# Two heads in the two halves of the partitions: float32r query and key parts for the shared-key and layer 2 attention

## The chip, the cores and the metric

The kernel runs on one core of one Trainium2 chip. The metric is the device time of one execution in microseconds (us); the median of some runs is compared.

## The reference, cut to what matters

A network of four layers works on x of 1024 tokens by 256 features, in float32. Three of its attentions are causal softmax attentions with 16 heads of 16 features: the latent attention of layer 0 (with rotated parts, 80 features per head), the shared-key attention beside it, and the attention of layer 2. The change touches the last two:

```python
# layer 0, feed-forward place: one key head for all query heads
att = einsum('bhqd,bkd->bhqk', q, k_shared) * (1.0 / sqrt(hd))
att = softmax(where(causal, att, -inf)); y = einsum('bhqk,bkd->bhqd', att, v_shared)
# layer 2
scores = einsum('bhqd,bhkd->bhqk', q, k) * scale
attn = softmax(where(causal, scores, finfo.min)); out = einsum('bhqk,bhkd->bhqd', attn, v)
```

## The kernel before, in words

Tokens are 8 tiles of 128 (T = 1024, P = 128, NT = 8, HALF = 512); a group is 4 heads (GH = 4, HD = 16). Groups 0 to 3 are the latent attention, 4 to 7 the shared-key one, 8 to 11 layer 2's. Each group goes through these steps.

- Row maxima. For each tile of queries TensorE makes approximate scores, queries on the PSUM partitions, keys along the bank (`maxima_unit`, L1553), adds a causal mask of bf16 with an identity (L1555), and VectorE reduces the bank (`row_maxima`, L1109). `MAX_UNITS` lists these units of at most 512 columns: 38 per group, with 4 heads of 128, 2 heads of 256 or 1 head of more columns. During attention they take turns in the 2 banks of psD; outside it (WIDE) in 4 banks. The negated maxima are transposed (L1561), copied (`mrow`, `mrowb`) and loaded by a DMA as one more row of the queries, against a row of ones in the keys.
- Scores. For each tile kt of keys, `score_units` makes the transposed scores of the 4 heads into psA (2 units of 2 banks, `scores_T`, L1571; the latent attention has a second product, L1570). For kt below 4 a unit is one head with both halves of the queries; from 4 on it is two heads with one half. ScalarE takes the exponential of each unit into Pr (L855, L860), GpSimd clears the triangle on the diagonal for the whole kt (`mask_exponentials`, L730).
- Values product. Four heads stand in four column groups of the array (`values_product`, L1608), one kt behind the scores. ScalarE copies psO to OT (L875) at the end of a group, TensorE transposes it (L1619), and VectorE divides and stores (`outputs`).

The maxima of group g are made beside the scores of groups g-1 and g-2, some units after each score unit or values product (`beside`, `some_maxima`), all of group 4's beside group 3. For groups 0 and 8 they are made ahead. TensorE works its list in order, so it waits where a bank isn't drained.

For groups 4 to 11 each query or key value is cut in three bf16 thirds (`split` on VectorE, `split_step` on GpSimd: copy, subtract, copy, subtract; L1101 to L1104), stored to DRAM (`d_gq`, `d_gk`, `d_q2`, `d_k2`), and loaded as 6 stacked products of parts, 96 rows, by `load_group`. The sixth-part order is

```python
Q_PARTS = (0, 0, 0, 1, 1, 2)
K_PARTS = (0, 1, 2, 0, 1, 0)
STACK = len(Q_PARTS) * HD
```

The latent attention keeps float32r parts (Qr, Kr), and its maxima read only the high bf16 halves of them (`high`). SyncE issues all DMAs in one order: group loads wait for the last scores of the group whose place they take.

## Time and profile before

| | |
|---|---|
| runs (3), us | 1019.24, 1023.3, 1026.06; median 1023.3 |
| profiled execution: span from first to last instruction | 1016.6 us (its own time isn't given beside the span) |
| TensorE busy | 868.2 us (85%) |
| VectorE, ScalarE, GpSimd busy | 572.4, 381.3, 225.2 us |
| mean granted TensorE clock | 0.910 of full |
| groups end (copy of psO begins), us | 199.74, 250.56, 302.16, 347.51, 381.48, 420.18, 454.16, 481.36; layer 2: 736.90, 770.75, 801.86, 823.16 |

### The profile page before, as it was taken

The page shows a single profiled execution, that of the slowest core. Times are in us where ns is not written, and L with a number is a line of the kernel's source. Part 1 is how long each engine was busy: PE and PEld are TensorE (multiplying, and loading weights), DVE is VectorE, ACT ScalarE, POOL GpSimd, SP SyncE. Part 2 cuts the span into 40 slices and gives each one's busy share as a digit, 9 for nine tenths or more (in the row PEclk, how much of TensorE's full clock was granted, in tenths as well). Part 3 has the DMA queues.
Part 4 walks back from the last instruction along what each step waited for, and adds up shares of the span by engine and source line. Part 5 has one row for each costly group of instructions (what it writes and reads, how often), then busy time and mean ns, then how long its engine had stood idle before and what let it go on. Part 6 is the DMA issues. An engine that isn't in the chain of part 4 may idle for free.

```text
span 1016.6 us, 11900 instructions
## 1 busy us (share of the span) xinstructions
PE 868.2 (85%) x4799; PEld 506.2 (50%) x4799; DVE 572.4 (56%) x986; ACT 381.3 (38%) x470; POOL 225.2 (22%) x207
## 2 busy tenths in 40 slices
PE   4991979788899999988589998978999889969897
PEld 2451335444455433334237877623333257868776
DVE  4871656363647777832543345396777427954452
ACT  2410014424243555465242331214555763410331
POOL 2541422401010234111210100400111227810010
PEclk9975679989899999999687998966999989989799
DMA  5599446374833400001500002477100051000001
GB/s 170 194 200 195 198 83 116 66 123 122 128 53 100 64 1 1 2 1 33 183 0 1 1 1 86 103 146 106 23 2 1 1 196 63 1 1 1 1 1 42
DMA packets 33313, 71.32 MB, mean 70 GB/s; under 512 B 5637, under 2 KB 14413, under 8 KB 33254
## 3 DMA queue, kind: packets, MB, share of 16 engines
q1 hardware_dynamic: 33258, 70.56, 30.1%
q8 instruction: 38, 0.62, 0.3%
q14 instruction: 17, 0.14, 0.0%
HBM read 49.27 MB, written 18.48 MB: 67 GB/s over the span
## 4 chain that ended last, share of the span: by engine, by line
PE 63%; DVE 19%; DMA 6%; ACT 5%; issue 4%; SPq 2%; POOL 1%; ACTq 0%; DVEq 0%; POOLq 0%
PE psD L1489 10%; PE psO L1608 10%; PE psO L1489 10%; PE psA L1489 9%; PE psD L1553 9%; DVE mx L1109 8%; PE psA L1571 7%; PE psA L1570 3%; DMA Kr<-d_kn 2%; DVE hid_low L1403 2%; SPq L460 2%; PE psD L1555 2%; ACT Pr L855 2%; PE psA L1521 1%; DVE Kg L1391 1%
## 5 line engine op out<-in xcount | busy, mean ns | idle before, releaser
L1109 DVE TENSOR_REDUCE mx<-psD 128x1 f32<-128x512 f32 (+3 forms) x416 | 258.0, 658 | 157.5 <-PE psD L1555 133.1
L855 ACT ACTIVATE Pr<-psA 128x1024 f32<-128x1024 f32 (+3 forms) x192 | 161.5, 865 | 167.5 <-PE psA L1571 167.0
L730 POOL TENSOR_SCALAR_AFFINE_SELECT Pr<-Pr 128x512 f32<-128x512 f32 x96 | 61.1, 636 | 402.8 <-ACT Pr L855 323.7
L860 ACT ACTIVATE Pr<-psA 128x1024 f32<-128x1024 f32 (+3 forms) x96 | 63.3, 702 | 60.3 <-PE psA L1571 59.9
L1608 PE MATMUL psO<-Pr,Vh 128*32 128x512 f32 (+3 forms) x768 | 80.3, 498 | 3.6 <-POOL Pr L730 3.0
L1553 PE MATMUL psD<-Kr,Qr 80*128 80x512 bf16 (+3 forms) x167 | 51.3, 360 | 35.7 <-issue 20.5
L1555 PE MATMUL psD<-maskq,identb 128*128 128x128 bf16 x349 | 72.5, 232 | 0.0
L1571 PE MATMUL psA<-Qr,Kr 113*128 113x512 f32 (+3 forms) x192 | 67.8, 359 | 0.0
L1553 PE MATMUL psD<-Kg,Qs 96*128 96x512 bf16 (+3 forms) x192 | 57.2, 331 | 5.3 <-DVE mx L1109 2.0
L1553 PE MATMUL psD<-Ks,Qs 96*128 96x512 bf16 (+3 forms) x166 | 54.5, 358 | 4.6 <-DVE mx L1109 3.7
L1553 PEld LDWEIGHTS psD<-Kr,Qr 80*128 80x128 bf16 x167 | 17.1, 105 | 75.6 <-issue 29.5
L1571 PE MATMUL psA<-Qs,Ks 97*128 97x512 bf16 (+3 forms) x192 | 46.7, 337 | 3.9 <-ACT Pr L855 3.3
L1521 PE MATMUL psA<-identf,xn 128*128 128x128 f32 x96 | 21.7, 389 | 31.5 <-DVE xn L1077 31.1
L1571 PE MATMUL psA<-Qs,Kg 97*128 97x512 bf16 (+3 forms) x192 | 44.9, 326 | 3.8 <-ACT Pr L855 3.3
L1553 PEld LDWEIGHTS psD<-Kg,Qs 96*128 96x128 bf16 x192 | 18.1, 96 | 54.9 <-DVE mx L1109 43.5
L1608 PE MATMUL psO<-Pr,Vg 128*32 128x512 f32 (+3 forms) x384 | 40.1, 497 | 2.0 <-POOL Pr L730 1.3
L1570 PE MATMUL psA<-Qr2a,Kr 128*128 128x512 f32 (+3 forms) x96 | 38.8, 418 | 3.2 <-issue 2.7
L1553 PEld LDWEIGHTS psD<-Ks,Qs 96*128 96x128 bf16 x166 | 16.7, 102 | 47.4 <-DVE mx L1109 41.5
L1571 PEld LDWEIGHTS psA<-Qr,Kr 113*128 113x128 f32 x192 | 38.0, 198 | 2.7
L1555 PEld LDWEIGHTS psD<-maskq,identb 128*128 128x128 bf16 x349 | 36.7, 105 | 4.9 <-issue 1.4
L1570 PE MATMUL psA<-Qr2b,Kr 128*128 128x512 f32 (+3 forms) x96 | 37.3, 402 | 0.6 <-ACT Pr L855 0.6
L1521 PEld LDWEIGHTS psA<-identf,xn 128*128 128x128 f32 x96 | 16.6, 195 | 35.5 <-issue 23.5
(392 smaller groups left out, 1730.0 us busy)
## 6 DMA issues: line engine op xcount, KB each, us to landing
d_qr<-Pr SPq DMA_DIRECT2D x16, 512.0 KB, 3.6
Qr<-d_qr SPq DMA_DIRECT2D x4, 1024.0 KB
Qr2a<-d_qr SPq DMA_DIRECT2D x4, 1024.0 KB, 24.9
Qr2b<-d_qr SPq DMA_DIRECT2D x4, 1024.0 KB, 19.9
Pr<-d_cb SPq DMA_DIRECT2D x8, 512.0 KB, 9.0
Qr<-d_qn SPq DMA_DIRECT2D x12, 256.0 KB, 13.6
Kr<-d_kn SPq DMA_DIRECT2D x12, 256.0 KB, 16.9
Qs<-d_gq SPq DMA_DIRECT2D x24, 128.0 KB
```

What stands on the lines that cost most here:

```text
L460: sp.dma_start(dst, src).then_inc(s, 16)
L730: pool.affine_select(out=block_, in_=block_, pattern=[[0, GH], [1, P]], compare_op=ALU.is_ge, fill=0.0, base=0, channel_multiplier=-1).the ...
L855: act.activation(place[:, h, q0:T], src[:, q0:T], ACT.Exp, scale=score_scale(i)).then_inc(a_drained, 1)
L860: act.activation(place[:, h:h + 2, q0:T], src[:, :, q0 - HALF:HALF], ACT.Exp, scale=score_scale(i)).then_inc(a_drained, 1)
L1109: dve.tensor_reduce(mx[:, j, part, h0:h0 + nh], src, AX, ALU.max).then_inc(d_drained, 1)
L1489: op = pe.matmul(dst, lhsT, rhs, start=start and k == 0, stop=stop and k == len(terms) - 1)
L1521: op = pe.transpose(dst[:, tile_cols(j)], src[:, j, c * P:(c + 1) * P], identf[:])
L1553: op = pe.matmul(dst[:, k * w:(k + 1) * w], q, kk, start=True, stop=not diagonal)
L1555: op = pe.matmul(dst[:, (k + 1) * w - P:(k + 1) * w], identb[:], maskq[:], start=False, stop=True)
L1570: pe.matmul(out_, second[0], second[1](lo, (half + 1) * HALF), start=True, stop=False)
L1571: op = pe.matmul(out_, k, q(lo, (half + 1) * HALF), start=second is None, stop=not (diagonal and mask))
L1608: op = pe.matmul(psO[h * VW:(h + 1) * VW, lo:hi], values(i, kt, h), e, start=kt == 0, stop=kt == last_kt, tile_position=(0, h * VW), skip_ ...
```

## The change

Queries and keys of groups 4 to 11 are kept as two float32r parts (ScalarE copies the value twice out of PSUM, once rounded to float32r; one subtraction gives the low part), and stacked three times (high by high, high by low, low by high): 48 rows, 49 with the row of maxima. Even heads stand in partitions 0 to 48, odd heads in 64 to 112. The shared key is held twice, once in each half. A score unit is now two heads (one of each half) and one half of the queries, each head in its own bank, for every kt. A maxima unit holds heads of one partition half only: the list for these groups is `PAIR_UNITS`, 40 units, heads alternating between halves. Maxima read the high bf16 halves of the float32r parts. The mask is added by two matmuls with 64 rows and 64 columns each from `mask64`, in the head's partition half. Stores to DRAM are two of 512 KB per tile in place of one of 768 KB; group loads have as many bytes, in rows of 4 KB in place of 2 KB; ones and maxima rows are loaded once for each half. The maxima row is float32r.

```diff
-Q_PARTS = (0, 0, 0, 1, 1, 2)
-K_PARTS = (0, 1, 2, 0, 1, 0)
+Q_PARTS = (0, 0, 1)
+K_PARTS = (0, 1, 0)
+ROWS = P // 2
+def pair_units():
+    for j in range(NT):
+        for part in range(1 + (j >= NT // 2)):
+            w = min(HALF, (j + 1) * P) if part == 0 else (j + 1) * P - HALF
+            for heads in ((0, 2), (1, 3)) if w <= 2 * P else ((0,), (1,), (2,), (3,)):
+                yield j, part, heads, w
...
-            o = ((i % 4) * GH + h) * T
-            return t[:].bitcast(BF16)[0:rows, o + a:o + b]
+            r, o = ROWS * (h % 2), ((i % 4) * GH // 2 + h // 2) * T
+            return (Qr if t is Qs else Kr)[r:r + rows, o + a:o + b]
...
+            for a in range(2):
+                load(mask64[a * ROWS:(a + 1) * ROWS, :, :],
+                     ins["c_maskk"].bitcast(BF16).rearrange("(c r) q -> r c q", c=2), consts_in)
...
                 def parts(t, d, order):
-                    for r, part in enumerate(order):
-                        load(t[:].bitcast(BF16)[r * HD:(r + 1) * HD, o:o + GH * T].rearrange("p (h t) -> p h t", h=GH),
-                             d[part, rows, :].rearrange("(h d) t -> d h t", d=HD), s)
+                    for a in range(2):
+                        for r, part in enumerate(order):
+                            at = a * ROWS + r * HD
+                            load(t[at:at + HD, o:o + n].bitcast(F32).rearrange("p (k t) -> p k t", k=GH // 2),
+                                 d[part, rows, :].rearrange("(k a d) t -> a d k t", a=2, d=HD)[a], s)
...
+            def store_parts(d, rows, u, n):
+                low, high_part = split_place(u)
+                for part, place in enumerate((high_part, low)):
+                    load(d[part, rows, :], place[0:rows.stop - rows.start], split_stored[n])
...
             def split(u, filled, rows=P, done=split_done):
                 pool.wait_ge(a_drained, filled)
-                for k in range(4):
-                    split_step(u, k, rows, done)
+                v, high_part = split_place(u)
+                pool.tensor_tensor(v[0:rows].bitcast(F32R), v[0:rows], high_part[0:rows], ALU.subtract).then_inc(done, 1)
...
-                        if kt < NT // 2:
+                        if kt < NT // 2 and not is_mla(i):
+                            for half in range(2):
+                                lo = max(q0, half * HALF)
+                                for h in range(0, GH, 2):
+                                    src = take().rearrange("p (h t) -> p h t", h=2)
+                                    act.activation(place[:, h:h + 2, lo:(half + 1) * HALF],
+                                                   src[:, :, lo - half * HALF:HALF], ACT.Exp,
+                                                   scale=score_scale(i)).then_inc(a_drained, 1)
...
+            def split_unit(u, rows=P):
+                src = take()[0:rows, :]
+                low, high_part = split_place(u)
+                act.activation(low[0:rows], src, ACT.Copy)
+                act.activation(high_part[0:rows].bitcast(F32R), src, ACT.Copy).then_inc(a_drained, 1)
...
-                link(dve.tensor_copy(b[:, 0], v))
-                link(dve.tensor_tensor(v, v, b[:, 0], ALU.subtract))
-                link(dve.tensor_copy(b[:, 1], v))
-                dve.tensor_tensor(b[:, 2], v, b[:, 1], ALU.subtract).then_inc(split_done, 1)
+                v, high_part = split_place(u)
+                dve.tensor_tensor(v.bitcast(F32R), v, high_part, ALU.subtract).then_inc(split_done, 1)
...
+            def maxima_unit(i, j, part, heads, w):
+                dst = d_unit()
+                rows = MLA if is_mla(i) else STACK
+                diagonal = part == (j >= NT // 2)
+                for k, h in enumerate(heads):
+                    q = high(head_rows(Qs, i, h, rows, j * P, (j + 1) * P))
+                    kk = high(key_rows(i, h, rows, part * HALF, part * HALF + w))
+                    end = (k + 1) * w
+                    op = pe.matmul(dst[:, k * w:end], q, kk, start=True, stop=not diagonal)
+                    if diagonal and is_mla(i):
+                        op = pe.matmul(dst[:, end - P:end], identb[:], maskq[:], start=False, stop=True)
+                    elif diagonal:
+                        half = slice(ROWS * (h % 2), ROWS * (h % 2 + 1))
+                        for c in range(2):
+                            at = end - P + c * ROWS
+                            op = pe.matmul(dst[:, at:at + ROWS], mask64[half, c, :], identb[half, half],
+                                           start=False, stop=c == 1)
...
+                def pair(unit):
+                    half, first = unit
+                    dst = a_unit()
+                    for b, h in enumerate((first, first + 1)):
+                        op = scores_T(dst, b * HALF, key_rows(i, h, rows, kt * P, (kt + 1) * P),
+                                      lambda lo, hi: head_rows(Qs, i, h, rows, lo, hi), kt, half)
+                    op.then_inc(a_filled, 1)
+
+                if not is_mla(i):
+                    return [(half, h) for half in range(kt * P // HALF, 2) for h in range(0, GH, 2)], pair
```

## Rows read from the trace of the kernel before

**Rows 1.** The page, the chain that ended last: shares of the span by engine.
```profile
PE 63%; DVE 19%; DMA 6%; ACT 5%; issue 4%; SPq 2%; POOL 1%; ACTq 0%; DVEq 0%; POOLq 0%
```

**Rows 2.** Windows: from:to, length, busy us of each engine (x instructions), granted clock, DMA share, GB/s.
```profile
347.50:381.50 34.00, 31.41 (x234) 12.35 (x233) 25.68 (x45) 19.41 (x27) 10.75 (x16) 1.00 0.17 22
692.50:736.90 44.40, 40.43 (x270) 16.40 (x270) 31.99 (x54) 24.93 (x30) 5.09 (x8) 0.90 0.50 73
801.90:823.20 21.30, 17.96 (x142) 5.35 (x142) 6.57 (x9) 15.38 (x23) 5.09 (x8) 1.00 0.00 1
677.60:692.00 14.40, 12.30 (x41) 3.78 (x41) 12.93 (x24) 0.00 (x0) 0.00 (x0) 0.50 0.15 58
765.90:771.66 5.76, 5.27 (x37) 2.09 (x36) 5.49 (x10) 4.79 (x6) 0.64 (x1) 1.00 0.00 0
```

**Rows 3.** The chain by line, first in group 4 (347.5:381.5), then in group 3 (302.2:347.5).
```profile
by line: PE psO L1608 24.3%; PE psD L1553 22.1%; DVE mx L1109 17.7%; PE psA L1571 15.5%; PE psD L1555 3.9%; POOL Pr L730 3.8%; PE psD L1619 3.4%; ACT Pr L860 3.2%; issue 2.5%; ACT Pr L855 2.4%; PE psD L1561 0.8%; DVE mneg L1114 0.8%; POOLq 
...
by line: PE psD L1553 24.9%; PE psO L1608 19.6%; PE psA L1571 16.6%; PE psA L1570 14.6%; DVE mx L1109 13.3%; DMA Qs<-d_gq 11.7%; PE psD L1555 5.5%; PE psD L1619 2.6%; issue 1.0%; PE psD L1561 0.2%
```

**Rows 4.** Timeline of VectorE in group 10: start, us, line [idle before, releaser].
```profile
773.39 1.89 DVE L1109 TENSOR_REDUCE mx<-psD 128x1 f32<-128x512 f32 x3 [0.63 <-PE psD L1553]
```

**Rows 5.** Timeline of TensorE in group 5: maxima, mask, then one values product.
```profile
382.49 0.22 PE L1553 MATMUL psD<-Kg,Qs 96*128 96x128 bf16 x1
382.55 0.22 PE L1555 MATMUL psD<-maskq,identb 128*128 128x128 bf16 x1
382.69 1.06 PE L1608 MATMUL psO<-Pr,Vg 128*32 128x512 f32 x8
```

**Rows 6.** Instructions by line and form: busy us, mean ns of one, idle before.
```profile
L1571 PEld LDWEIGHTS psA<-Qr,Kr 113*128 113x128 f32 x192 | 38.0, 198 | 2.7
...
L1571 PEld LDWEIGHTS psA<-Qs,Kg 97*128 97x128 bf16 x192 | 15.6, 98 | 22.2 <-ACT Pr L855 10.1 <-issue 2.8 <-ACT Pr L860 1.7
...
L1571 PE MATMUL psA<-Qr,Kr 113*128 113x128 f32 x32 | 8.2, 275 | 0.0
...
L1571 PE MATMUL psA<-Qs,Kg 97*128 97x128 bf16 x32 | 5.3, 221 | 1.9 <-ACT Pr L855 1.8
```

**Rows 7.** Timeline of TensorE at 38.9, at 514.4 and at 266.3 us.
```profile
38.90 0.50 PE L1489 MATMUL psO<-lat_parts,wq_low 64*128 64x512 f32 x1
39.33 0.50 PE L1489 MATMUL psO<-lat_parts,wq_high 128*128 128x512 f32 x1
...
514.42 0.23 PE L1774 MATMUL psD<-K,Q 32*128 32x128 bf16 x1
514.58 0.23 PE L1777 MATMUL psD<-maskq,identb 128*128 128x128 bf16 x1
...
266.33 0.39 PE L1570 MATMUL psA<-Qr2a,Kr 128*128 128x512 f32 x1
266.56 0.39 PE L1571 MATMUL psA<-Qr,Kr 113*128 113x512 f32 x1
```

**Rows 8.** The chain before group 8, and ScalarE's timeline there (the last row).
```profile
642.62 1.24 DVE Pr L1102
...
649.72 3.44 DMA d_k<-Pr
...
653.59 0.43 SPq L460
...
659.72 7.32 DMA Ks<-in_c_ones4b
...
644.27 1.02 ACT L822 ACTIVATE Pr<-psA 128x1024 f32<-128x1024 f32 x1 [2.41 <-PE psA L1489]
```

**Rows 9.** Windows in which the DMAs are full: 2 KB rows, then 4 KB rows.
```profile
654.00:666.00 12.00, 7.58 (x45) 6.61 (x44) 7.07 (x19) 3.93 (x10) 8.38 (x5) 0.91 1.06 149
194.00:205.00 11.00, 5.30 (x28) 3.37 (x26) 0.00 (x0) 5.71 (x6) 3.39 (x4) 0.92 1.01 165
```

More of the change, by code:

```diff
@@ L74, in max_units, with units_of @@
                 yield j, part, h0, nh, w
-MAX_UNITS = list(max_units())
+MAX_UNITS = [(j, part, tuple(range(h0, h0 + nh)), w) for j, part, h0, nh, w in max_units()]
+def pair_units():
[4 more added lines that the diff above has]
+                yield j, part, heads, w
+PAIR_UNITS = list(pair_units())
+def units_of(g):
+    return MAX_UNITS if g < NG else PAIR_UNITS
 MAX_END = 5
@@ L159, in build @@
         mrow = sb("mrow", [GH * NT, P])
-        mrowb = sb("mrowb", [GH * NT, P], BF16)
+        mask64 = sb("mask64", [P, 2, P], BF16)
         rec = sb("rec", [P, 4, GH])
@@ L337, in maxima_of, with rows_in @@
             return 2 * NG + 1 if i == "L1" else maxima(i)
+        ROW_DMAS = [1] * NG + [2] * NG + [1] + [2] * NG
+        def rows_in(count):
+            return 16 * sum(ROW_DMAS[:count])
         A_GROUP = 4 * GH + 4 * GH // 2
@@ L535, in maxima_row @@
                 else:
-                    o = (i % 4) * GH * T
-                    load(Qs[:].bitcast(BF16)[STACK:STACK + 1, o:o + GH * T], mrowb[:], mrow_in)
+                    o, n = (i % 4) * GH // 2 * T, GH // 2 * T
+                    for a in range(2):
+                        at = a * ROWS + STACK
+                        load(Qr[at:at + 1, o:o + n].bitcast(F32), mrow[a * n // P:(a + 1) * n // P, :], mrow_in)
             for p in range(H // 2):
@@ L749, in _ @@
                     mask_exponentials(i, kt)
-                    if i == 0:
-                        split_step(kt // 4, kt % 4)
+                    if i == 0 and kt % 4 == 0:
+                        split(kt // 4, A["gq"])
                     n = NT * (i - NG) + kt
@@ L953, in _ @@
                 if u == 3:
[L954 to L955 removed]
+                    act.wait_ge(split_stored[0], 32 * 2)
+                split_unit(3 + u)
             act.wait_ge(v_cleared, 4)
@@ L1183, in attention @@
                             maxima_row(nxt)
-                        row_maxima(beside(groups, i, kt)[1])
+                        row_maxima(*beside(groups, i, kt))
                         if kt == 1 and i - 1 in groups:
@@ L1540, in value_units @@
                         last.then_inc(d_filled, 1)
-            def maxima_unit(i, j, h0, nh, w, part):
+            def maxima_unit(i, j, part, heads, w):
                 dst = d_unit()
                 rows = MLA if is_mla(i) else STACK
-                for k in range(nh):
-                    h = h0 + k
-                    q = head_rows(Qs, i, h, rows, j * P, (j + 1) * P)
-                    kk = key_rows(i, h, rows, part * HALF, part * HALF + w)
-                    if is_mla(i):
-                        q, kk = high(q), high(kk)
-                    diagonal = part == (j >= NT // 2)
-                    op = pe.matmul(dst[:, k * w:(k + 1) * w], q, kk, start=True, stop=not diagonal)
-                    if diagonal:
-                        op = pe.matmul(dst[:, (k + 1) * w - P:(k + 1) * w], identb[:], maskq[:], start=False, stop=True)
+                diagonal = part == (j >= NT // 2)
[12 more added lines that the diff above has]
+                                           start=False, stop=c == 1)
                 op.then_inc(d_filled, 1)
@@ L1632, in attention @@
                     arrived(groups[0])
-                    for j, part, h0, nh, w in MAX_UNITS:
-                        maxima_unit(groups[0], j, h0, nh, w, part)
+                    for unit in units_of(groups[0]):
+                        maxima_unit(groups[0], *unit)
                     maxima_transpose(groups[0], GH)
```

138 lines of the change are left out of this document (64 added, 74 removed).

## The prediction

> **What bounds the kernel now.** I read the page's chain that ended last first: TensorE holds 63% of it and VectorE 19% [rows 1]. Then I cut the attention into its groups of four heads, each ending with the copy of psO by ScalarE. Groups 0 to 3 are the first attention, 4 to 7 the shared-key one, 8 to 11 layer 2. In [rows 2] the reader is to see that no engine fills a group: group 4 takes 34.0 us with VectorE busy 25.7 and ScalarE 19.4, and group 9 repeats it (33.8 us); groups 5, 6, 7 and 10 (38.7, 34.0, 27.2 and 31.2 us by the table of their ends) are of the same make with other work beside.
>
> The chain inside group 4 says who is late: values products (L1608) 24.3%, maxima matmuls (L1553) 22.1%, VectorE's maxima 17.7%, scores (L1571) 15.5%, masks (L1555) 3.9% [rows 3]. So scores are 5.3 us of a group's 34.0, maxima matmuls 7.5, masks 1.3. Nor is the time one kind of time. The first eighth of a group (kt 0) lasts 5.76 us with VectorE busy 5.49: there nothing but VectorE counts. After it VectorE waits 0.6 us at a time for TensorE to come back from a values product [rows 4]. That is the time a faster TensorE can take.
>
> **Overlap of the halves.** Now a score matmul uses 97 rows, one head at a time; after, 49 rows of one half, the next head in the other half, into another PSUM bank. No row of before shows two matmuls on different rows of the array. The nearest show them on different columns: eight values products of 512 columns, four heads at a time, end within 1.06 us, and 128 columns alone keep a matmul 0.22 us [rows 5]; so tiles do run together. The bounds: a pair costs as much as one (5.3 us become about 2.7 per group), or as much as two (no gain). I take the first, by that row, with 0.2 us lost because a float32r score is up to 54 ns longer than a bf16 one (275 against 221 ns at 128 columns [rows 6], less where more columns hide the weight load): -2.5 us. Maxima matmuls alternate halves too, but only 2 psD banks take turns and VectorE empties them, so two of them seldom meet; one can run beside half of a score pair. Between 0 and -2.5 us (a third of 7.5); I take -0.8, since VectorE takes most of that back.
>
> **What the same groups lose.** (a) 32 diagonal heads per group get two mask matmuls of 64 columns for one of 128. Mask and maxima matmuls of 128 columns start 0.06 us apart [rows 5]; two halves cost between nothing more and 0.06 each, so 0 to 1.9 us per group; I take 0.2, as columns rule in all the rows. (b) Maxima read high halves in steps of four bytes; no row parts that from the rest, so I bound it at 0 and 5% of their 7.5 us, and take 0.2. (c) Tile mode. A switch is seen at both ends of a values product: its first matmul starts 0.14 us after a mask matmul, where 0.06 is usual [rows 5]. These switches stay. Where 128-row and 64-row float32r matmuls alternate, starts are 0.43 us apart at 512 columns [rows 7], against 0.23 between two float32r matmuls of 128 and 113 rows; where bf16 matmuls of 32 and 128 rows alternate, 0.16 us against 0.06 [rows 7]. So a switch costs 0.1 us, 0.2 when a float32r weight load follows. The output transposes (128 rows) now stand between 64-row work: two switches, +0.3. (d) Float32r weight loads last 198 ns, bf16 ones 98 [rows 6]; behind a short mask matmul they show, +0.3. (e) Two more maxima units, 40 for 38: +0.2. Sum of losses 1.2 us, so group 4, 5 and 9 gain 2.1 each: -6.3. After it VectorE's 25.7 us plus its waits are next late; at 31.9 us there is room. Group 8 has the same scores, but more of it is VectorE's (32.0 of 44.4 us [rows 2]): -2.0. Groups 6 and 10 have fewer maxima to fill: -1.2 each. Groups 7 and 11 have none; there a score follows each values product directly and pays the float32r switch (about 0.1 us, 6 to 9 times), and the chain runs through ScalarE and GpSimd: -0.3 each.
>
> On that weight load the Trainium skill (TensorE: Matmul & The Clock Gate, Weight-path perf modes) speaks against the change: fast weight load is on for 128 weights of a type other than FP32. The trace agrees in direction, by the 198 against 98 ns. And (TensorEngine Tiling (Array Packing), Key Properties) it says that a change of tiling mode drains TensorE; the trace agrees, with the 0.43 us starts. Neither page prices the two; by the rows they are the 0.3 and 0.3 us of (c) and (d), and without them the sum would be some 4 us lower.
>
> **Group 3.** It scores the first attention (113 and 128 rows) while it makes the maxima of group 4. These maxima now have 48 rows, so each of some 15 changes from maxima to scores costs 0.15 more (a float32r load after a switch, less the 0.05 paid already) and some 14 back 0.1: 3.6 us. Part of it falls where TensorE waits for a bank anyway. +2.5; the bounds are 0 and 3.6, and it is TensorE that leads this chain (L1553, L1608, L1571 and L1570 hold 76% [rows 3]).
>
> **Around the groups.** Before group 8 the chain runs through four VectorE steps for each of two tiles, which end at 649.7 us, the store of d_k2 (3.44), 12 loads issued at some 0.45 us each, and the landing at 667.0 [rows 8]. After: ScalarE copies twice (1.02 us more), VectorE subtracts once. ScalarE takes the second tile from 644.3 on, and two copies and one step of 1.24 us end near 644.3 + 2.1 + 1.2 = 647.6: -2.1. The stores grow from 0.75 to 1.0 MB: +0.7. One more load of ones and a second DMA for the maxima row, each 0.4 of issue: +0.8. The loads carry the same bytes but 4 KB rows for 2 KB; in stretches where the DMAs are full, 4 KB rows moved 165 GB/s and 2 KB rows 149 [rows 9], so the 13.4 us of loading shrink by 1.3 (between 0 and 3). Together -1.9. VectorE's run of 38 maxima after it is as long as before, within 0.2. The load of group 4, waited for in group 3 (11.7% of its chain [rows 3]), gains by the same rate, -0.5. GpSimd's splits of four steps become one subtraction; in group 0, where they stand between the selects, I count nothing, since selects hold under 4% of a chain [rows 3]. The two loads of mask64 are issued ahead of the first projections and hidden by x and the norm. The longer ScalarE drains (two copies) sit under TensorE's 3.4 us per unit.
>
> **Sum.** -6.3 - 2.0 - 2.4 - 0.6 + 2.5 - 1.9 - 0.5 = -11.2 us. The span of 1016.6 becomes 1005.4. The profiled execution's own time isn't shown beside the span; the median of the runs is 1023.3, 6.7 us more, so I add 6.7: 1012.1 us.
>
> **Rivals.**
> A, turns: the two halves do not run together. For it: no row shows row tiles together. Against it: the column tiles [rows 5]. Place: every score pair. Then a strong group pays the 1.2 us of losses and 0.6 for longer float32r scores instead of gaining: +1.8 in 4, 5, 8 and 9, +1.3 in 6 and 10, +1.0 in 7 and 11, +2.5 in group 3, -2.4 around: +11.9, 1035 us, slower. It decides from the point where a pair of 512 columns costs more than one and a half matmuls.
> B, weight loads in turn: the halves stream together but float32r loads do not. At 128 columns the float32r score lasts 275 ns against 221 [rows 6], which is the load showing. Eight of a group's 24 pairs have 256 columns or fewer and four have 384; they would cost some 0.1 and 0.05 more, 1.0 per group in six groups: 1018 us.
> C, the clock: where TensorE is fed at VectorE's pace, the granted clock is 0.50, the 1.2 GHz level (677.6 to 692.0 us [rows 2]), and it stays so into group 8. If less TensorE work lets it fall in the VectorE-bound start of groups too, each fall costs about 3 us (half of TensorE's share of some 6 us), six times: 1030 us. Against it: group 11, with TensorE least busy, keeps 1.00, the 2.4 GHz level [rows 2].
> D, more overlap: maxima matmuls hide as well, and groups fall to VectorE's time plus 4.5 us of waits, 30 us; -3.8 in three groups, as much in proportion elsewhere, and 4 KB rows pay fully: 1001 us.
> That the change does nothing of what it says is A.
>
> **Chances.** The sum 0.47 (1006 to 1018), A 0.12, B 0.14, C 0.12, D 0.15. The range of 999 to 1031 leaves out most of A and the tail of D. A measurement here can tell about 1%, from 1013.1 to 1033.5. Faster by more: D, two thirds of the sum's case and little of B, 0.49. Slower: A and a tail of C, 0.13. Within: 0.38.
>
> **What would show it.** Right: two L1571-like matmuls starting within 0.02 us in different halves; scores under 9% of a strong group's chain; groups 4 and 9 near 32 us; group 3 near 48 us without its DMA wait shrinking much; group 8's first maxima near 665 us; a few tenths of a microsecond between 64-row and 128-row matmuls in group 3. Wrong: pairs starting 0.2 us apart (A), pairs of 128 columns 0.2 us apart (B), clock under 1.00 in groups 4 to 7 (C). The forecast is most open in how much of the overlap VectorE gives back, and in group 3.

## The result and the profile after

The changed kernel takes 1082.1 us, median of 4 executions (1076.9 to 1089.3), beside 1023.8 for the kernel before: ratio 1.059, 95% interval 1.055 to 1.062. The profiled span is 1087.5 us against 1016.6, 70.9 more; it is that of the longest of the four executions, so it lies further from before than the medians do, which are 58 apart. The prediction of 1012 has the wrong sign, and 1082 is outside its range of 999 to 1031. In this document medians are over all executions of a kernel, and ratios over those that lie near its fastest, because a kernel whose clock dips scatters by several per cent.

The page of the changed kernel: TensorE's row of busy time, then the clock in 40 slices, then the chain by engine, which answers to [rows 1].

```profile
PE 929.4 (85%) x5055; PEld 543.8 (50%) x5055; DVE 567.6 (52%) x996; ACT 388.1 (36%) x477; POOL 205.1 (19%) x192
...
PEclk9985789898999566789688998855656888989898
...
PE 66%; DVE 16%; DMA 6%; ACT 5%; issue 4%; SPq 2%; POOL 1%; DVEq 0%; ACTq 0%
```

The row to read is PEclk: from slice 14 on, in the shared-key groups, it shows 5 to 8 for the most part where the groups of before had 1.00 throughout, and again in layer 2. Windows of the changed kernel, columns as in [rows 2]: group 4, group 8 from 1.8 us behind its first score (the window of before in [rows 2] begins 0.6 us ahead of that score, so the two lengths don't compare), group 9, group 11, then key tile 1 and key tile 4 of group 4.

```profile
356.43:402.35 45.92, 43.43 (x267) 19.15 (x265) 26.55 (x46) 19.42 (x27) 10.72 (x16) 0.57 0.12 16
733.00:785.58 52.58, 49.13 (x304) 21.67 (x302) 32.73 (x55) 23.04 (x29) 5.09 (x8) 0.56 0.45 57
785.58:831.15 45.57, 43.23 (x267) 19.56 (x265) 26.55 (x46) 19.39 (x27) 5.08 (x8) 0.57 0.01 1
865.20:890.77 25.57, 21.18 (x142) 6.87 (x142) 6.57 (x9) 15.44 (x22) 5.09 (x8) 0.80 0.00 1
357.33:367.87 10.54, 10.40 (x55) 4.45 (x54) 5.80 (x12) 3.57 (x6) 1.94 (x3) 0.50 0.42 53
381.98:385.19 3.21, 3.06 (x34) 1.38 (x34) 2.34 (x5) 1.93 (x4) 2.50 (x4) 1.00 0.00 0
```

Group 4 takes 45.9 us instead of 34.0 while VectorE (26.6 us busy for 25.7) and ScalarE have almost the same work as before. TensorE is busy 43.4 of it, and its granted clock is 0.57, the mean of stretches at 0.50 (1.2 GHz) and at 1.00 (2.4 GHz). Key tile 1 runs wholly at 0.50 with TensorE busy 10.40 of 10.54 us; key tile 4, at 1.00, takes 3.2 us. Group 11, at 1.00 before, has 0.80.

The same by line, group 4 first, then group 3, beside [rows 3].

```profile
by line: PE psO L1644 34.8%; PE psD L1571 26.0%; PE psA L1595 15.5%; DVE mx L1131 10.2%; PE psD L1578 4.9%; PE psD L1655 4.1%; ACT Pr L867 2.2%; issue 1.6%; PE psD L1585 0.6%; DVE mrow L1148 0.6%; DVE mneg L1136 0.6%; DVEq L1065 0.1%
...
by line: PE psD L1571 22.9%; PE psA L1594 18.1%; PE psO L1644 17.8%; DVE mx L1131 15.7%; PE psA L1595 13.6%; DMA Qr<-d_gq 10.8%; PE psD L1578 4.6%; PE psD L1655 2.3%; issue 1.6%; DVE mrow L1148 0.6%; PE psD L1585 0.2%; DVEq L1065 0.1%
```

The values products (L1644), which the change does not touch, go from 24.3% of 34.0 us to 34.8% of 45.9, from 8.3 us to 16.0: the mark of a slower clock, not of more work. VectorE's share falls from 17.7% to 10.2%. TensorE bounds the group.

The overlap itself is there. TensorE's timeline in key tile 4 of group 4, at the full clock: four score products of 384 columns, in two pairs, are over in 0.60 us; in the kernel before, four in turn took 0.81 (fourth row). But it does not reach short products: four of 128 columns in two pairs take 0.44 us (fifth row, group 7 of the changed kernel), four in turn took 0.39 (last row, group 4 of before).

```profile
384.37 0.41 PE L1571 MATMUL psD<-Kgr,Qr 48*128 48x512 bf16 x2
384.61 0.23 PE L1578 MATMUL psD<-identb,mask 64*128 64x64 bf16 x4
384.67 0.60 PE L1595 MATMUL psA<-Qr,Kgr 49*128 49x384 f32 x4
...
368.65 0.81 PE L1571 MATMUL psA<-Qs,Kg 97*128 97x384 bf16 x4
...
514.43 0.44 PE L1595 MATMUL psA<-Qr,Kgr 49*128 49x128 f32 x4
...
374.52 0.39 PE L1571 MATMUL psA<-Qs,Kg 97*128 97x128 bf16 x4
```

By the copies of psO, the 70.9 us of span lie so: groups 4, 5 and 9 +12.0, +11.3 and +11.7; group 8 from its first score to its end +10.5; group 3 +5.4; groups 6, 7, 10 and 11 +2.0, +2.3, +2.9 and +4.3; the way from group 7 to group 8's first score +1.7; groups 0 to 2 +3.5 and all behind group 11 +3.3. The 3.5 us come and go from kernel to kernel: that of experiment 5, which leaves these groups as they were, has 3.7 of them.

The way into group 8 in the chain, beside [rows 8], and the window in which its loads fill the DMAs, beside the first of [rows 9].

```profile
685.12 3.55 DMA d_k<-Pr
...
694.80 9.86 DMA Kr<-onesf
...
705.35 21.88 DVE mx L1131 x40
...
729.05 2.15 DMA Qr<-mrow
```

```profile
690.00:704.00 14.00, 8.84 (x53) 7.77 (x52) 4.49 (x21) 4.33 (x11) 2.35 (x1) 0.90 1.06 143
```

From the end of the last split (684.7 us; 649.7 before), when the first of the two stores is issued, to the landing of the loads (704.7; 667.0) it is 19.9 us, 17.3 before. With 4 KB rows the loads moved 143 GB/s, with 2 KB rows 149.

### The profile page after: what moved, and what is told of

Its sections match the earlier page's. It is cut to its first block, busy times and chain, and to the rows that moved or that the text cites. A ratio compares the mean times of both kernels' runs of the same rounds, so it can differ in the third digit from the quotient of the medians.

```text
span 1087.5 us, 12430 instructions
## 1 busy us (share of the span) xinstructions
PE 929.4 (85%) x5055; PEld 543.8 (50%) x5055; DVE 567.6 (52%) x996; ACT 388.1 (36%) x477; POOL 205.1 (19%) x192
## 4 chain that ended last, share of the span: by engine, by line
PE 66%; DVE 16%; DMA 6%; ACT 5%; issue 4%; SPq 2%; POOL 1%; DVEq 0%; ACTq 0%
PE psO L1644 13%; PE psD L1509 10%; PE psD L1571 9%; PE psA L1509 9%; PE psO L1509 9%; DVE mx L1131 7%; PE psA L1595 7%; PE psA L1594 3%; DMA Kr<-d_kn 2%; SPq L465 2%; DVE hid_low L1423 2%; ACT Pr L867 2%; PE psA L1541 1%; PE psD L1578 1%; DMA Pr<-d_cb 1%
## 5 line engine op out<-in xcount | busy, mean ns | idle before, releaser
L1131 DVE TENSOR_REDUCE mx<-psD 128x1 f32<-128x512 f32 (+4 forms) x432 | 264.2, 643 | 210.9 <-PE psD L1573 88.2
L1571 PE MATMUL psD<-Kr,Qr 80*128 80x512 bf16 (+7 forms) x335 | 121.5, 414 | 45.9 <-issue 21.9
L1595 PE MATMUL psA<-Qr,Kr 49*128 49x512 f32 (+7 forms) x384 | 130.6, 470 | 6.2 <-ACT Pr L867 4.4
L1571 PEld LDWEIGHTS psD<-Kr,Qr 80*128 80x128 bf16 (+1 forms) x335 | 34.4, 106 | 140.1 <-DVE mx L1131 60.1
L1644 PE MATMUL psO<-Pr,Vh 128*32 128x512 f32 (+3 forms) x768 | 99.9, 606 | 2.8 <-POOL Pr L740 2.3
L1595 PEld LDWEIGHTS psA<-Qr,Kr 113*128 113x128 f32 (+1 forms) x384 | 69.3, 225 | 24.4 <-ACT Pr L867 11.6
L1571 PE MATMUL psD<-Kgr,Qr 48*128 48x512 bf16 (+3 forms) x192 | 68.8, 411 | 7.8 <-DVE mx L1131 4.3
L1595 PE MATMUL psA<-Qr,Kgr 49*128 49x512 f32 (+3 forms) x192 | 58.4, 553 | 4.3 <-ACT Pr L867 3.5
L1644 PE MATMUL psO<-Pr,Vg 128*32 128x512 f32 (+3 forms) x384 | 55.7, 670 | 1.7 <-POOL Pr L740 1.3
L1578 PE MATMUL psD<-identb,mask 64*128 64x64 bf16 x480 | 56.8, 220 | 0.0
L1578 PEld LDWEIGHTS psD<-identb,mask 64*128 64x128 bf16 x480 | 48.9, 116 | 14.9 <-issue 8.2
L1509 PE MATMUL psA<-xnT,WA 128*128 128x512 f32 x56 | 30.9, 712 | 2.2 <-ACT xnT L832 2.2
```

Source lines behind the costliest of these rows:

```text
L1131: dve.tensor_reduce(mx[:, j, part, max_slots(i, heads)], src, AX, ALU.max).then_inc(d_drained, 1)
L1509: op = pe.matmul(dst, lhsT, rhs, start=start and k == 0, stop=stop and k == len(terms) - 1)
L1571: op = pe.matmul(dst[:, k * w:end], q, kk, start=True, stop=not diagonal)
L1578: op = pe.matmul(dst[:, at:at + ROWS], mask64[half, c, :], identb[half, half], start=False, stop=c == 1)
L1595: op = pe.matmul(out_, k, q(lo, (half + 1) * HALF), start=second is None, stop=not (diagonal and mask))
L1644: op = pe.matmul(psO[h * VW:(h + 1) * VW, lo:hi], values(i, kt, h), e, start=kt == 0, stop=kt == last_kt, tile_position=(0, h * VW), skip_ ...
```

## The experiments

Fifteen kernels ran, one of them twice. Each is a small edit of one of the two kernels; "clock" is the granted clock of whole groups in the windows of its trace.

**1. Score pairs in turn.** The pair takes two heads of one half.

```diff
-                    for b, h in enumerate((first, first + 1)):
+                    for b, h in enumerate((first // 2, first // 2 + 2)):
```

> The changed kernel, but the two score products of a pair take heads (0,2) or (1,3), which lie in the same half of the partitions, so that they run one behind the other; products, columns, maxima and masks are the same, and ScalarE writes the same numbers. Theory A (the clock falls because the pairs run at once and leave TensorE too lightly loaded): the granted clock of groups 4, 5, 8 and 9 returns from 0.56 to 0.64 towards 1.0, and the time falls from 1082 to 1025 to 1050 us although the overlap is lost. Theory B (the clock falls because the maxima use half of the rows, whatever the scores do): the clock stays at 0.55 to 0.65 and the time rises by the lost overlap, 5 us a group at the lower level, to 1095 to 1120. Theory C (the time is in mode switches and weight loads, the clock is a symptom): time up by 2.5 us a group, about 1100.

1132.5 us, ratio 1.107 (1.099 to 1.114). The clock in groups 4, 5 and 6 was 0.57, 0.67 and 0.69, group 4 took 48.3 us. So the overlap is not what lowers the clock (theory A falls), and the kernel is 50 us slower without it. That is not the overlap alone: group 4, at 0.57 with and without it, loses 2.4 us, while groups 6, 10 and 11 also have a lower clock than in the changed kernel (0.69, 0.67 and 0.56 against 0.88, 0.85 and 0.80).

**2. Full-array work ahead of each pair.**

```diff
                     dst = a_unit()
+                    for c in range(4):
+                        pe.matmul(dst[:, c * P:(c + 1) * P], identb[:], maskq[:], start=True, stop=True)
```

> The changed kernel with idle work added: ahead of each score pair TensorE multiplies four full 128 x 128 tiles by 128 columns into the bank that the pair then overwrites, 192 times 0.23 us = 44 us of TensorE at the full clock, 89 us at the lower one. Nothing is left out. The clock theories (A or B): the full-array work lifts the granted clock of groups 4, 5, 8 and 9 above 0.85, so their 45 to 50 us go to 36 to 42 and the whole kernel does not get slower, 1050 to 1085 us, with 44 us of TensorE work more. Rival C (mode switches and TensorE work bound it): the clock stays near 0.6 or does not matter, and the time goes up by 45 to 90 us, 1125 to 1170.

1153.9 us (1126.5 to 1166.9). Groups 4 and 5 in the windows of an execution of 1162.7 us:

```profile
358.85:412.63 53.78, 51.87 (x364) 24.40 (x363) 26.76 (x48) 19.98 (x27) 10.68 (x16) 0.70 0.08 11
412.63:458.30 45.67, 43.23 (x371) 21.35 (x369) 30.71 (x57) 19.87 (x26) 14.78 (x14) 0.97 0.01 2
```

Neither reading was wholly right. The time is where rival C put it; the clock did not stay near 0.6 everywhere: one group holds 0.97, the next falls to 0.62, and TensorE's added work costs more than the clock gives back. In this trace group 5, at 1.00 in its first key tile, keeps it, while groups 4 and 6 are down to 0.50 by key tile 1 and stay there for two key tiles or more.

**3. Maxima over 112 rows.** The masks are whole again too; the score pairs still run at once.

```diff
-                rows = MLA if is_mla(i) else STACK
+                rows = MLA if is_mla(i) else ROWS + STACK
...
+                    hh = h if is_mla(i) else h - h % 2
```

> The changed kernel, but the maxima products contract 112 rows instead of 48: rows 48 to 63, filled with the second parts by one DMA more for each of the tiles, and the other half are taken in, so each product is of two heads together and the maxima are not the reference's; the masks are 128 x 128 again. The score pairs still run at once. Theory A (the overlap of the scores pulls the clock down): the clock stays at 0.6 to 0.75, time 1055 to 1085 us. Theory B (the half-array maxima do): the clock of groups 4, 5, 8 and 9 is above 0.9 and the time near 1020 to 1035. Theory C (switches): four switches a key tile fewer, 1060 to 1075 with the clock as low as before.

> The changed kernel with maxima products of 112 rows, once more, for its trace: 1051 us again. Theory B (the half-array maxima hold the clock down): groups 4, 5 and 9 at a granted clock of 0.9 or more, so that what is left of the loss, 29 us, is float32r weight loads, turns between tiles at the scores, and the lead-in to group 8. Theory A (the score pairs hold it down as well): still 0.6 to 0.8 in some of these groups.

1051.4 us, ratio 1.027 (1.024 to 1.031); one of its four executions took 3713.7 us, of which more at the end. The kernel was run once more and took 1047.7, and the windows are of that execution. Groups 4 and 9:

```profile
356.70:392.53 35.83, 33.68 (x235) 12.58 (x233) 26.27 (x47) 19.47 (x26) 10.74 (x16) 1.00 0.13 21
762.40:798.15 35.75, 33.70 (x235) 12.55 (x233) 26.27 (x47) 19.39 (x26) 5.07 (x8) 1.00 0.01 2
```

With full-array maxima and masks the clock is back at 1.00, although the pairs still run in half tiles (groups 7 and 11, without maxima, have 0.86 and 0.89). Theory B holds for the larger part of the loss. And a second finding: at the full clock group 4 still takes 35.8 us, 1.9 more than before.

**4. Half-array maxima in the kernel before.**

```diff
-                rows = MLA if is_mla(i) else STACK
+                rows = MLA if is_mla(i) else 48
...
+                            op = pe.matmul(dst[:, at:at + 64], mask64[0:64, c, :], identb[0:64, 0:64],
```

> The kernel before, but its maxima products contract the first 48 of the 96 rows, and the mask products are in two parts of 64 rows as in the changed kernel; the scores are the old ones of 97 rows, one head at a time. Maxima leave out the second and third parts of the query. Theory A (only overlapped scores pull the clock down): clock 0.95 to 1.0 in groups 4, 5 and 9, time 1025 to 1040 us. Theory B (half-array maxima do): clock 0.55 to 0.7 in groups 4, 5, 8 and 9, time 1070 to 1090. Theory C (switches between row tiles of 64 and 128 cost the time): 1045 to 1060 with the clock near 1.0.

1128.3 us (1102.9 to 1138.6), though the scores are the old ones. Groups 4 and 10 of the execution of 1102.9 us:

```profile
357.69:409.81 52.12, 50.70 (x268) 15.91 (x267) 26.65 (x45) 19.77 (x27) 10.66 (x16) 0.63 0.09 12
833.49:883.23 49.74, 48.03 (x217) 13.31 (x216) 18.55 (x32) 19.52 (x26) 5.10 (x8) 0.56 0.00 1
```

Cause and effect from the other side: half-array maxima with their cut masks, put into the old kernel, cost 81 us at its fastest and 106 at the median. They do not lower the clock everywhere: groups 5 and 6 of this trace have 1.00.

**5. Few rows, or the half tile?** Maxima of 65 rows in the kernel before.

```diff
-                rows = MLA if is_mla(i) else STACK
+                rows = MLA if is_mla(i) else 65
```

> The kernel before, but its maxima products contract the first 65 of the 96 rows: one row more than half of the array, so that they remain products of a 128-row tile beside the scores of 97 rows, and no mask is cut in two. Left out of the maxima: the second and third parts of the query. Theory B1 (few active rows in the maxima keep the clock low; 48 rows did): 65 rows do some of it, granted clock below 0.9 in at least two of the groups 4, 5, 8, 9, 10 and 1040 to 1090 us. Theory B2 (what keeps the clock low is the half-array row tile and what comes with it, the turns between 64-row and 128-row tiles): clock 1.0 in groups 4, 5, 9 and 10 and 1020 to 1026 us, as before.

1024.7 us, ratio 1.004 (1.001 to 1.007), group 4 in 33.99 us at 1.00. Leaving out a third of the rows does no harm as long as the products are no half tiles. A bound between 48 and 65 active rows that had nothing to do with tiles would look the same; no run parts these two.

**6. No half tiles at all.** Maxima and scores over 112 rows.

```diff
+                        hh = h - h % 2
+                        op = scores_T(dst, b * HALF, key_rows(i, hh, ROWS + STACK, kt * P, (kt + 1) * P),
```

> The changed kernel with no 64-row tile in the shared-key and layer 2 attention: maxima and scores contract 112 rows, of two heads together, one product behind the other, so the output is not the reference's; columns, exps, transfers and the float32r operands of the scores are those of the changed kernel. Theory B (64-row tiles hold the clock down): groups 4, 5, 8, 9 and 10 at 1.0 as before, 1018 to 1035 us, the rest over 1022 being float32r weight loads and the lead-in to group 8. Rival (float32r score products, with their 4-byte operands, hold it down): clock 0.6 to 0.8 and 1055 to 1090 us.

1044.0 us, ratio 1.023 (1.018 to 1.027), clock 1.00 in groups 4, 5, 6 and 9; group 4 takes 35.84 us. The first theory is right on the clock, but the time is above the 1035 that it allowed. In group 4 it ties with the 112-row kernel of experiment 3, in which the pairs run at once (35.83 us). So there the overlap gains nothing over full tiles in turn. TensorE's timelines show why. First the kernel of experiment 5, whose scores are those of before, then this one, that of experiment 3 and that of experiment 7 below, each with a maxima product, the pair, and the next maxima product:

```profile
349.31 0.39 PE L1553 MATMUL psD<-Kg,Qs 65*128 65x512 bf16 x1
349.54 0.60 PE L1571 MATMUL psA<-Qs,Kg 97*128 97x512 bf16 x2
349.97 0.90 PE L1553 MATMUL psD<-Kg,Qs 65*128 65x512 bf16 x2
...
436.88 0.39 PE L1578 MATMUL psD<-Kgr,Qr 112*128 112x512 bf16 x1
436.91 0.82 PE L1596 MATMUL psA<-Qr,Kgr 112*128 112x512 f32 x2
437.57 0.40 PE L1578 MATMUL psD<-Kgr,Qr 112*128 112x512 bf16 x1
...
435.55 0.39 PE L1578 MATMUL psD<-Kgr,Qr 112*128 112x512 bf16 x1
435.87 0.49 PE L1596 MATMUL psA<-Qr,Kgr 49*128 49x512 f32 x2
436.30 0.40 PE L1578 MATMUL psD<-Kgr,Qr 112*128 112x512 bf16 x1
...
439.48 0.39 PE L1578 MATMUL psD<-Kgr,Qr 112*128 112x512 bf16 x1
439.80 0.73 PE L1596 MATMUL psA<-Qr,Kgr 49*128 49x512 f32 x2
440.46 0.40 PE L1578 MATMUL psD<-Kgr,Qr 112*128 112x512 bf16 x1
```

From one maxima product to the next it is 0.66 us with bf16 scores in turn, 0.69 with float32r scores of 112 rows in turn, 0.75 with half tiles at once, and 0.98 with half tiles in turn. So among half tiles the overlap does gain: the next product starts 0.43 us after a pair at once and 0.66 after a pair in turn. But half tiles in turn between full-tile products cost 0.29 more than full tiles in turn (0.98 - 0.69), and the overlap gives 0.23 of that back.

**7. Only the scores in half tiles, in turn** (experiments 1 and 3 together).

> The changed kernel with maxima products of 112 rows (two heads together) and the score pairs taken from one half, so that half-array products still run, but only the scores, and in turn. Theory B (what holds the clock down is any stretch in which one half-array product runs at a time): the granted clock of groups 4, 5, 8, 9 falls to 0.55 to 0.8 and the time is 1070 to 1110 us. Rival (the scores alone are too small a share of TensorE's time, or the turns between full and half tiles let it recover): clock 0.95 to 1.0, and the time is 1048 us plus the lost overlap, 3 us in each of eight groups: 1062 to 1075 us.

1089.9 us, ratio 1.063 (1.056 to 1.070). Clock 1.00 in groups 4 and 5 but 0.63 in group 7, which has scores and values products only:

```profile
354.49:393.42 38.93, 36.46 (x234) 14.72 (x233) 26.35 (x47) 19.60 (x26) 10.73 (x16) 1.00 0.12 18
474.13:514.55 40.42, 38.00 (x175) 16.73 (x174) 4.65 (x10) 15.50 (x22) 5.07 (x8) 0.63 0.03 10
```

Against experiment 3, running at once is worth 3.1 us in group 4 (38.93 against 35.83). Theory B expected a lower clock in groups 4, 5, 8 and 9, and they have 0.83 to 1.00; the rival's time, up to 1075, is passed, in part because groups 7 and 11 fall (0.63 and 0.81). Half-array scores, too, lower the clock where no full-array maxima stand between them.

**8. A burst of full-array work at key tile 1.**

```diff
+                    for _ in range(64 * (kt == 1 and unit == (0, 0))):
+                        pe.matmul(dst[:, 0:P], identb[:], maskq[:], start=True, stop=True)
```

> The changed kernel with 64 full-array products of 128 x 128 x 128 ahead of the first score pair of key tile 1 in each of the groups 4 to 11, 3.7 us at the full clock and 6.8 us at the lower one; their results are overwritten. Theory B (nothing but a stretch of full-array work lifts the clock, and the half-array maxima only fail to lift it): the clock returns during the burst and stays for the rest of the maxima, key tiles 1 to 3 of group 4 take 17 us in place of 24.7, groups 4, 5 and 9 take 40 to 43 us in place of 46 to 50, and the whole 1055 to 1080 us. Rival (half-array maxima pull a full clock down again within a key tile): clock back at 0.50 in key tile 2, groups 50 us or more, whole 1110 to 1140 us.

1085.5 us, ratio 1.060 (1.053 to 1.067): as the changed kernel, and between the two forecasts. Four windows of group 4, of about a key tile each, cut at the first exp of each; the burst is in the first:

```profile
350.04:360.57 10.53, 9.75 (x103) 7.16 (x102) 5.75 (x10) 4.90 (x6) 1.34 (x2) 0.84 0.94 144
360.57:367.63 7.06, 6.28 (x60) 2.94 (x57) 5.56 (x11) 3.56 (x5) 1.34 (x2) 1.00 0.01 3
367.63:372.73 5.10, 4.62 (x42) 1.86 (x38) 4.35 (x8) 3.15 (x4) 0.00 (x0) 1.00 0.01 2
372.73:378.48 5.75, 5.48 (x34) 2.01 (x34) 3.42 (x7) 2.62 (x4) 1.34 (x2) 0.70 0.00 0
```

Full-array work does lift the clock, and half-array maxima pull it down again: 0.70 in key tile 3 here, 0.57 in key tile 2 of the next group. The second and third rows are the changed kernel at the full clock: 7.06 and 5.10 us, where the kernel before, cut in the same way, has 7.37 and 5.16. Key tile 4 follows at 1.00 as well, with 3.15 us against 3.70. That is what the change gains there when the clock holds: 0.9 us in three of the eight key tiles.

**9. One maximum for two heads.** Half of the maxima units, over 112 rows and with whole masks as in experiment 3.

```diff
-            for heads in ((0, 2), (1, 3)) if w <= 2 * P else ((0,), (1,), (2,), (3,)):
+            for heads in ((0, 2),) if w <= 2 * P else ((0,), (2,)):
```

> The changed kernel, but what the softmax subtracts is, for the two heads of a pair, the maximum of the sum of their scores: one maxima product of 112 rows for two heads, half as many products, masks and row maxima, and the negated maxima written twice. The row maxima of each head by itself are left out; the softmax divides the same factor out again, so the output stays near the reference's while that sum does not lie far below a head's own scores. Expected by the full-clock reading of the 112-row kernel (1048 us): TensorE loses 8 us of maxima products and 3 us of masks in each of eight groups, and VectorE 10 us; ScalarE's 19 to 20 us a group and the values products are left. Groups of 36 us become 27 to 30 us, the lead-in to group 8 loses 10 us: 975 to 1000 us, under both kernels. Theory A (half-tile scores alone hold the clock down once the full-array maxima get fewer): clock 0.6 to 0.8 and 1020 to 1050 us.

1010.4 us, ratio 0.986 (0.978 to 0.994), one or two per cent under before but above the forecast. Two executions took 1004 us and one 1017; the fourth took 1309.5, with a mean granted clock of 0.548, so this kernel isn't safe from a long fall of the clock either. Group 4 takes 32.1 us at 0.89 and group 6 34.8 at 0.84: the clock still dips in an ordinary execution. It is no drop-in: what it subtracts is the maximum of a sum of two heads' scores, which bounds neither head, and the exp can overflow on other data.

**10 and 11. Which part of the half-array maxima?** Maxima of 48 rows with whole masks, then whole maxima with cut masks, both in the kernel before: of the two added lines of experiment 4, the first alone, then the second alone.

> The kernel before with maxima products of 48 rows, its masks left in one product of 128 rows (the earlier kernel of this kind cut them as well, and took 1128 us). Left out of the maxima: the second and third parts of the query. Theory B (half-array maxima hold the clock down): clock 0.55 to 0.8 in at least three of groups 4, 5, 8, 9 and 10, 1070 to 1125 us, although the mask products now bring full-array work in between. Rival (the cut masks did it): clock 0.95 to 1.0; the time is 1022 us plus the turns into and out of the half tile at the diagonal units, 4 us in each of eight groups: 1050 to 1060 us.

1183.9 us (1166.3 to 1194.1). Groups 5 and 9:

```profile
431.59:496.47 64.88, 64.38 (x244) 17.56 (x243) 31.26 (x55) 19.77 (x26) 14.69 (x14) 0.57 0.00 1
852.47:914.91 62.44, 61.98 (x235) 15.75 (x235) 26.93 (x45) 19.88 (x27) 5.10 (x8) 0.53 0.00 1
```

> The kernel before with only its mask products cut into two of 64 rows and 64 columns; maxima and scores have 96 and 97 rows as before and nothing is left out. Theory B: half-array work is now 5 us of a group of 34 us, so the clock stays at 0.95 to 1.0, and the time is 1022 us plus the turns between tiles around 32 mask products a group: 0.1 us in and 0.15 us out, half of it beside VectorE's row maxima: 1045 to 1075 us. Rival (the cut masks are what holds the clock down): clock 0.6 to 0.8, 1090 to 1130 us.

1086.3 us, ratio 1.061 (1.052 to 1.071). Groups 9 and 6:

```profile
787.32:835.95 48.63, 47.80 (x266) 15.81 (x265) 26.36 (x45) 19.56 (x26) 5.10 (x8) 0.71 0.00 1
448.46:484.10 35.64, 32.33 (x231) 12.22 (x230) 18.47 (x33) 20.95 (x28) 5.10 (x8) 1.00 0.00 1
```

Half-array maxima do it without cut masks, and worse than theory B allowed (up to 1125); that each mask is now a turn between tile sizes may be why. But the cut masks alone do it as well, in part, which theory B excluded: 0.71 in group 9, 0.79 in group 4, yet 1.00 in group 6. So the share of half-array work is not the whole of it, and three more runs went to the turns.

**12, 13 and 14. Turns by themselves.** One short product, 64 columns wide, ahead of each maxima unit: of 64 rows and of 128 rows in the kernel before, of 128 rows in the changed one.

```diff
+                if not is_mla(i):
+                    pe.matmul(dst[:, 0:64], identb[0:64, :], maskq[0:64, 0:64], start=True, stop=True)
```

> The kernel before with one product of 64 rows by 64 columns ahead of each of its maxima units of the shared-key and layer 2 attention (44 a group), overwritten by the unit. It adds hardly any half-array work (64 columns, 0.03 us), but a turn into the half tile and one out of it, measured at 0.10 and 0.07 us. Theory T (the array standing empty at the turns between tile sizes brings the clock down): granted clock 0.55 to 0.85 in groups 4, 5, 8 and 9 and 1080 to 1130 us. Theory S (the share of time in half-array products does): clock 0.95 to 1.0, time 1022 plus the turns, at most 7 us a group and half of them hidden: 1045 to 1075 us.

> The control of the run with 64 rows: the same extra product ahead of each maxima unit, but of 128 rows, so that there is no turn. Both theories: clock as before, 1.0 in groups 4, 5, 9 and 10, and at most 1.3 us a group: 1022 to 1034 us. Above 1045 us the extra instructions themselves, not the tile, would be the cause in both runs.

> The changed kernel with one product of 128 rows by 64 columns ahead of each of its 48 maxima units a group: hardly any work, two turns more per unit. Theory T (turns bring the clock down): worse than the changed kernel, clock 0.5 to 0.6 through groups 4 to 10, 1110 to 1170 us. Theory S (the share of half-array time, hardly changed): clock as in the changed kernel, 0.56 to 0.9, and 1082 plus 5 to 8 us a group of turns at the lower clock: 1110 to 1145 us. They differ most in groups 6, 7 and 10: by theory T these fall below 0.75.

1066.6 us, ratio 1.042 (1.035 to 1.048); 1029.9, ratio 1.007 (1.004 to 1.010); 1200.3, ratio 1.171 (1.162 to 1.179). Group 4 of each, in this order:

```profile
359.93:398.76 38.83, 37.56 (x273) 15.09 (x271) 26.38 (x45) 19.43 (x27) 10.71 (x16) 1.00 0.11 16
```

```profile
349.50:384.26 34.76, 32.51 (x272) 13.65 (x271) 25.86 (x46) 19.39 (x27) 10.74 (x16) 1.00 0.19 23
```

```profile
374.60:433.72 59.12, 58.83 (x308) 24.91 (x307) 27.43 (x47) 19.82 (x26) 10.72 (x16) 0.50 0.06 8
```

Turns alone leave the clock at 1.00 (theory S holds in the kernel before) and cost 38.83 - 34.76 = 4.1 us a group. Added to half-array maxima, they come with a clock of 0.50 from end to end of group 4, and 0.57 and 0.50 in groups 6 and 10: there theory T's clocks came out, but for group 7 (0.85), and the time passed even its range, up to 1170. So half-array maxima and turns together do more than either alone. How they do it is not shown.

**15. Filler in the shared-maximum kernel.**

> The kernel with one maximum for two heads (1004 to 1017 us) with two full-array products of 128 columns ahead of each score pair, 24 pairs a group, 2.8 us a group at the full clock, overwritten. Left out: the row maxima of each head by itself. If full-array work at the entry of the half-tile pairs holds the clock up: groups 6, 7, 10 and 11 at 1.0, each 3 to 5 us shorter, against 2.8 us of added work half hidden under ScalarE: 990 to 1003 us. Rival (two more idle-free products do not stop the falls, as 4 did not in the changed kernel): 1020 to 1035 us.

1016.5 us, ratio 0.993 (0.988 to 0.997); one of its ten executions took 4139.5 us. Group 4 is now at 1.00 and takes 32.0 us, as without filler; group 11 is still at 0.76. The filler buys the clock back in part and costs as much. No version with half tiles got under the kernel before without leaving work out.

## Why the prediction was wrong

**The step that failed** is that the sum holds no term for the clock. It priced every product at the durations of before, which hold at 2.4 GHz. Rival C named the mechanism, with the wrong place and size: it let the clock fall in the VectorE-bound start of groups, six times, 3 us each, 18 us in all. The runs show it falling in stretches of half-array products, and staying down with TensorE busy 99% of a key tile. Its evidence against, that group 11 keeps 1.00 with TensorE least busy, spoke of idle time and not of half-array products. How much of the 58 us is the clock's can be bounded from below by experiment 3, which takes 1048 to 1051 with the clock mostly back: 31 to 34 us. What exactly brings the clock down stays open (experiments 10 to 14).

**Overlap, -2.5 a group.** That the halves run together was right. The size was not: by the ends of the rows, four products in two pairs save 0.21 us of 0.81 at 384 columns and 0.10 of 0.60 at 256, lose 0.05 at 128, and a pair of 512 saves 0.11 of 0.60. A group has two such fours of each of the shorter widths and twelve pairs of 512, which gives an estimate of 1.8 us a group at most, for 2.5. The 3.1 us of experiment 7 against 3 is the overlap's worth against half tiles in turn, which are themselves slower than the scores of before.

**Tile mode, +0.3 and "these switches stay".** In the changed kernel maxima, masks and scores are all half tiles, so turns are few. Where half tiles stand between full ones (experiment 7 against 6) a pair costs 0.29 us more, which is what the 0.1 and 0.2 of the prediction add up to for a way in and out; how much of it is the turns themselves the rows don't part. Around the short product of experiment 12 it is 0.11 (4.1 us with 38 units in group 4), part of it hidden. The Trainium skill (TensorEngine Tiling (Array Packing), Key Properties) says that a change of tiling mode drains TensorE; the traces agree in direction, with these 0.29 us.

**Sum of the groups, -2.1 in 4, 5 and 9.** At the full clock, by experiment 8, key tiles 1, 2 and 4 of group 4 give 0.9 us together. Its group 9, at 0.95, takes 37.9 us, of which the burst is 3.7 by its forecast: 34.2 are left, where before had 33.85. So a gain of 2.1 doesn't show even near the full clock; no run shows a whole group of the changed kernel at 1.00, and whether the change would then have been a tie or a small gain stays open.

**Group 3, +2.5.** Measured +5.4. But experiment 6, without any turn there, has +4.4 (49.8 against 45.35 us). Its losses are therefore not the turns for the most part: half of them lie in key tile 1 (13.4 us against 11.2), where it waits for the tiles of group 4 and the clock dips to 0.87. The size is out by a factor of two and the reason mostly wrong. The 0.5 us that its load was to gain did not come either: the wait is 10.8% of 50.8 us, 5.5, and was 11.7% of 45.35, 5.3.

**Before group 8, -1.9.** Measured +1.7 up to the first score. The splits gained what was predicted, 2.2 for 2.1: the last one ends 35.0 us later than before where the end of group 7 is 36.4 later and the product that is split 0.8 more. Store, issues and loads together, with the second row of maxima, were to cost 0.2 us; up to the landing they cost 2.6 (19.9 against 17.3), and the way from there to the first score 0.5 more. 4 KB rows came at 143 GB/s and not at the 165 that I took. My two windows of [rows 9] differ in source and count as well as in the length of rows.

**Rival A** (turns) has the closest sum among the full-clock kernels: 1035 against 1044 to 1051. It would have been right in sign for the wrong reason. Rival B's price did come: two pairs of 128 columns take 0.44 us where four products in turn took 0.39, and a pair of 512 saves 0.11 us where a pair as cheap as one product would save some 0.22, the distance of two starts. That float32r weight loads are the reason (the four of 128 columns load for 0.30 us) is likely, but no run parts them from the rest. Rival D did not occur.

## What to carry to other kernels

Packing two products into two halves of the array did not pay here beside full-tile products: a pair cost 0.29 us more for being in half tiles and the overlap gave back 0.23. Nor does it pay for short float32r products (0.44 us for four of 128 columns against 0.39 in turn), and stretches of half-array products can bring the clock to 0.50. Where TensorE bounds a stretch, price a change of tile shape at both levels of the clock, and look at the granted clock of windows before looking at counts. If the operand fits in 65 rows or in 48, 65 may be the faster.

## What the runs showed of the hardware

- The granted clock stood at 0.50 with TensorE busy 10.40 of 10.54 us in the changed kernel, and 58.83 of 59.12 in experiment 14: by the profile a busy TensorE is not enough for 2.4 GHz.
- Maxima products of 65 rows in the place of 48 in the same kernel: 1024.7 against 1184 us.
- Work of like make ran at either level within one execution. In the trace of experiment 2 one group ran at 0.97 and the next at 0.62; in experiment 8 the key tiles after a burst stayed at 1.00, two in group 4 and one in group 5, before the clock fell.
- Two products of 384 columns in different halves, twice, were over in 0.60 us. Products of two halves that would write the same bank were not tried.
- The granted clock doesn't tell of every slow TensorE. In the execution of 3713.7 us of experiment 3 it reads 1.00, VectorE is busy 565.6 us as ever (567.6 in the changed kernel), and TensorE 3664.8: float32r products of 128 rows and 512 columns (L1515) take 3.08 us in the median instead of 0.59. Nothing in the trace says why.
- What tells cut masks (clock 0.71 in group 9) from the short half-tile products of experiment 12 (1.00), with about as many turns, stays open. The cut masks add to a result in the bank, and there are two for each; no run parts these.
